# First attention of a two-layer kernel: fixed places for its small steps and long products

## The reference

```python
xn = _layernorm(x)
q, k, v = (split_heads(xn @ W.T) for W in (Wq, Wk, Wv))      # 8 batches, 16 heads, width 16
scores = jnp.where(causal, (q @ k.T) / sqrt(16), -inf)        # 512 x 512 for each head
x = x + (softmax(scores) @ v).reshape(8, 512, 256) @ Wo.T + ffn(xn)
```

## Time and profile before

| | |
|---|---|
| median of 3 runs | 1774.12 us (1771.36 to 1778.27) |
| profiled execution | 1778.4 us, span 1776.6 us |
| first attention, from scoresT of head 0 to the end of output | 64.8 to about 547 us |
| TensorE busy | 1613.5 us (91%) |
| VectorE busy | 863.5 us (49%) |
| ScalarE busy | 677.2 us (38%) |
| GpSimd busy | 741.4 us (42%) |
| mean granted TensorE clock | 0.961 |

### The profile page before, as it was taken

How to read it: one execution, slowest core, us unless ns; L and a number is a source line. 1 busy time by engine, 2 the same in 40 slices (tenths; PEclk the granted TensorE clock), 3 DMA queues, 4 the chain that set the end, 5 groups by cost and what they waited for, 6 DMA issues and landing times.

```text
span 1776.6 us, 32082 instructions
## 1 busy us (share of the span) xinstructions
PE 1613.5 (91%) x10912; PEld 1207.1 (68%) x10912; DVE 863.5 (49%) x2460; ACT 677.2 (38%) x1680; POOL 741.4 (42%) x845
## 2 busy tenths in 40 slices
PE   6888978888889999999896689998999999999997
PEld 3445434444446899999554456556899999999996
DVE  6777786657641322332264999886322122222221
ACT  4444434445462222222452334432433333333332
POOL 3122235545531455554621258785233333333332
PEclk9789989989999999999998799999999999999999
DMA  8434234353605122222531464464522222222221
GB/s 250 93 111 108 63 73 82 73 91 73 109 11 201 54 69 72 72 70 68 183 109 35 134 158 105 86 96 114 218 38 37 35 41 37 37 37 37 37 37 22
DMA packets 80027, 149.99 MB, mean 84 GB/s; under 512 B 13220, under 2 KB 61472, under 8 KB 73920
## 3 DMA queue, kind: packets, MB, share of 16 engines
q1 hardware_dynamic: 55328, 110.56, 24.6%
q0 software_dynamic: 24544, 37.38, 9.6%
HBM read 103.05 MB, written 44.45 MB: 83 GB/s over the span
## 4 chain that ended last, share of the span: by engine, by line
PE 78%; DVE 11%; issue 4%; ACT 2%; POOL 2%; DMA 1%; DVEq 0%; SPq 0%; ACTq 0%; POOLq 0%
PE PS L1488 22%; PE PS L1506 21%; PE PS L1366 4%; DVE PS L1793 4%; PE PS L1599 3%; PE PS L1302 3%; PE PS L1420 3%; PE PS L1462 2%; PE PS L1690 2%; PE PS L1330 2%; PE PS L1351 2%; PE PS L1473 2%; PE PS L1312 2%; PE PS L1392 2%; PE PS L1609 1%
## 5 line engine op out<-in xcount | busy, mean ns | idle before, releaser
L1488 PEld LDWEIGHTS PS<-arena 128*128 128x128 f32 x3408 | 398.3, 192 | 15.8 <-DVE arena L2016 4.5
L1488 PE MATMUL PS<-arena 128*128 128x128 f32 x3408 | 405.4, 276 | 3.1 <-DVE arena L2016 3.1
L1506 PE MATMUL PS<-arena 128*128 x1704 | 392.3, 379 | 0.0
L1506 PEld LDWEIGHTS PS<-arena 128*128 128x128 f32 x1704 | 311.6, 190 | 40.2 <-issue 0.2
L2016 DVE COPY arena<-PS 128x256 f32<-128x256 f32 x142 | 60.3, 424 | 413.0 <-PE PS L1473 402.6
L1793 DVE CUSTOM_DVE_ANT_0 PS<-PS,arena 128x512 f32<-128x512 f32 (+3 forms) x512 | 234.2, 524 | 39.5 <-PE PS L1330 39.2
L901 POOL DMA_INDIRECT out<-arena x71 | 111.6, 1572 | 314.0 <-ACT arena L1152 292.7
L1142 ACT ACTIVATE arena<-PS,arena 128x128 f32<-128x128 f32 x568 | 161.8, 368 | 138.2 <-PE PS L1488 138.2
L1077 ACT ACTIVATE arena<-PS 128x512 f32<-128x512 f32 (+1 forms) x256 | 167.2, 705 | 75.4 <-PE PS L1351 73.0
L841 POOL TENSOR_SCALAR_AFFINE_SELECT arena<-arena 128x256 f32<-128x256 f32 x256 | 98.5, 410 | 224.2 <-ACT arena L1077 223.2
L887 POOL DMA_INDIRECT arena<-XN,arena x142 | 142.1, 1001 | 102.7 <-PE PS L1473 64.5
(11 more groups left out here) (242 smaller groups left out, 2020.9 us busy)
## 6 DMA issues: line engine op xcount, KB each, us to landing
arena<-FD SPq DMA_DIRECT2D x32, 512.0 KB
arena<-in_w SPq DMA_DIRECT2D x16, 1024.0 KB
SPL<-arena SPq DMA_DIRECT2D x32, 384.0 KB, 2.6
arena<-SPL SPq DMA_DIRECT2D x30, 384.0 KB
XN<-arena SPq DMA_DIRECT2D x16, 512.0 KB, 3.2
arena<-SUM SPq DMA_DIRECT2D x16, 512.0 KB, 5.0
arena<-SPL SPq DMA_DIRECT2D x30, 256.0 KB
arena<-SPL SPq DMA_DIRECT2D x34, 128.0 KB, 3.9
```

The lines of the kernel that those rows point to most:

```text
L1488: ins = pe.matmul(o, m.now[i % 2][:, c * F + 128 * f:c * F + 128 * f + 128], m.xt[i % 2][:, 128 * c:128 * c + 128], start=(c == 0), stop=( ...
L1506: ins = pe.matmul(to, m.hT[i % len(m.hT)][:, 128 * c:128 * c + 128], m.WD[:, bass.ds(e * (nf * 256) + c * 256, 256)], start=(c == 0), stop ...
```

## The change

`attention_places()` gives each small step and each long product a fixed idx, and a side: 0 behind scoresT, 1 behind scores. The queue, its ranks and its pauses are gone. `values`, the stacks, the norm, the routing and the scatters stay where they were by idx, and the number of steps is the same.

In the old list, in the steady state, counting idx modulo 16: output twice at 2 (once on each side), project_v twice at 3, project at 5 and 6 and at 13 and 14 (side 1), scale at 1, 6, 9 and 14 (side 0), unscaleT at 2 and 10 (side 0), split and maxrow at 5 and 13.

```diff
+def attention_places():
+    places = {}
+
+    def put(idx, behind, *steps):
+        places.setdefault((idx, behind), []).extend(steps)
+
+    for n in range(2, NHB):
+        first = -LEAD if n == 2 else 8 * n - (22 if n % 2 else 18)
+        put(first, 1, ("project", n, 0))
+        put(1 - LEAD if n == 2 else 8 * n - 17, 1, ("project", n, 1))
+    for n in range(NHB):
+        put(8 * n - 3, 0, ("split", n))
+        put(8 * n - 3, 1, ("maxrow", n))
+        for g in range(2):
+            put(8 * n + 4 * g + 5, 1, ("scale", n, g))
+        put(8 * n + 10, 0, ("unscaleT", n))
+    for b in range(NB):
+        put(16 * b + 19, 1, ("output", b, 0))
+        put(16 * b + 22, 1, ("output", b, 1))
+        if b:
+            put(16 * b - 6, 1, ("project_v", b, 0))
+            put(16 * b - 5, 1, ("project_v", b, 1))
+    put(NH + 1, 1, ("shared_up", 0, 3), ("shared_gelu", 0, 3))
+    put(NH + 3, 1, ("shared_up", 1, 0), ("shared_gelu", 1, 0))
+    return places
...
-            step(False)
+        out += places.pop((idx, 0), [])
+        lead = idx + LEAD
         if lead < NH:
             out.append(("scores", lead // 8, lead % 8))
-            if lead % 8 == 7:
-                later(0, [("pause",), ("split", lead // 8), ("maxrow", lead // 8)])
-        step()
...
+        out += places.pop((idx, 1), [])
+        if idx == 2 - LEAD:
+            out.append(("stack", 2))
+        if 4 <= idx <= NH and idx % 4 == 0:
+            g = idx // 4 - 1
...
+            out.append(("values", g // 2, g % 2))
```

More of the change, by code:

```diff
@@ L54, in ln0_steps @@
             yield [(kind, b)]
-def attention_order():
[L59 to L80, removed]
+def attention_places():
[21 more added lines that the diff above has]
+    return places
+def attention_order():
+    out, places, ln = [], attention_places(), ln0_steps()
     out += [("stats", 0), ("root", 0), ("norm", 0), ("xt0", 0), ("xt1", 0), ("stats", 1), ("root", 1), ("norm", 1)]
@@ L85, in attention_order @@
     out += [("stats", 2), ("stats", 4), ("logits", 0), ("logitsT", 0), ("stats", 3), ("logits", 1), ("logitsT", 1), ("stats", 5)]
-    later(0, [("project", 2, 0), ("project", 2, 1), ("stack", 2)])
     route = iter([("route", p) for p in range(20)] + [("scatter", i, (k,)) for i in range(NT) for k in range(2)])
@@ L89, in attention_order @@
     lnleft = True
-    for idx in range(-LEAD, NH + 1):
-        if idx % 8 == 5 and 3 <= (idx + 3) // 8 + 2 < NHB:
-            later(0, [("project", (idx + 3) // 8 + 2, 0), ("project", (idx + 3) // 8 + 2, 1), ("pause",)])
+    for idx in range(-LEAD, NH + 7):
         if idx % 8 == 0 and 3 <= idx // 8 + 2 < NHB:
@@ L102, in attention_order @@
             out += [("shared_gelu", 0, fc) for fc in range(3)]
-        lead = idx + LEAD
         if idx == 0:
@@ L107, in attention_order @@
             out.append(("scoresT", idx // 8, idx % 8))
-            step(False)
+        out += places.pop((idx, 0), [])
+        lead = idx + LEAD
         if lead < NH:
             out.append(("scores", lead // 8, lead % 8))
-            if lead % 8 == 7:
-                later(0, [("pause",), ("split", lead // 8), ("maxrow", lead // 8)])
-        step()
[L114 to L123, removed]
+        out += places.pop((idx, 1), [])
[3 more added lines that the diff above has]
+            g = idx // 4 - 1
+            if g >= 2 * NHB - 2:
+                out.append(("shared_up", 0, g - 2 * NHB + 3))
+            out.append(("values", g // 2, g % 2))
         if lnleft:
@@ L131, in attention_order @@
             out += [s for s in [next(clears, None)] if s]
[L132 to L137, removed]
+    assert not places
     out += list(route)
@@ L140, in attention_order @@
     return out
-CLOSE = ("stack", "maxrow", "unscaleT", "pause", "done")
 def shared_order():
```

## The result

The changed kernel takes 1763.43 us (median of 20 runs, 1753.3 to 1772.32), the kernel before in the same comparisons 1773.96 (20 runs, 1769.1 to 1780.39). The ratio is 0.9942 [0.9925, 0.9958], a gain of 10 us (10.5 by the medians) or 0.6% (0.4 to 0.75%). That is faster by about the bound of 0.5%, inside the range, and **half of the 20 us forecast**.

The account below looks back on a forecast made before the run. The order of the work, no engine always busy, was taken as the bound. Six windows at 3.1 (18.6 us), first window 2, last 1.1, routing -2: 20 us less, 1754 against 1774.1; own range 1745 to 1764, full range 1732 to 1778.

Parts of the forecast that it names:

- The walk of the steps: Step-by-step sum over sixteen heads of the first attention: 51 us against 55.3 before, 4.3 us less.
- unscaleT at 2: At position 2, unscaleT would wait about 1.2 us for the scaled rows, since VectorE does the row maxima first.
- Output at 6: At position 6, output follows scale in bank 7 and would wait 0.4 us for VectorE's read.
- Values at 8: With no projection ahead in POOL's queue, its wait at position 8 would fall from 2.6 to about 0.35, worth 2.2 us.
- Values at 4: At position 4, values would wait 0.7 us for the low part of the projection at 2, masks queued behind it.
- bare sum of 50.4: Sum of the sixteen walked steps, in us, before adding 0.1 to 0.2 for steps with a projection, which gave 51.
- the term of the stack: Ahead of a group's first scores, late stacks would cost 1.2 us per sixteen heads; ends 0 and 4.4 + 3.1.
- the routing window: Window of the routing steps: VectorE, busy 56 of 66 us, can give back only half of the gain; -2 us.
- The first window: First sixteen-head window: would gain about 2 us, since project_v leaves a step of 6.5 us.
- the rival called halved: Waits on VectorE come out near 2 us, 4.3 becomes 2.3 or less, the whole 10 us: 1764 to 1768; chance 0.22.
- the third rival: Stacks land late for each odd group, 4.4 us of stall, clock halving behind each: about 1805; chance 0.14.
- The first rival, the clock: TensorE keeps 2.4 GHz with shorter waits; some 4 us more per window in five windows: 1734; chance 0.18.

Follow-up runs that it names:

- e_noscat: Changed kernel with the 64 scatters moved out of the attention loop to after it; 1810.89 us, one execution, only the windows are compared.
- the three other executions named above: Profiled executions of e_after, e_noscat and e_gap, whose order up to head 48 is the changed kernel's; first window 62.8, 63.1 and 61.4 us.
- e_gap_scale_low: Changed kernel with scatters kept out of stack steps, scale(n, 1) ahead of the scores, and q's low part behind the next head's masks; 1739.72 us, ratio 0.9833.
- e_before_noscat: Kernel before with the 64 scatters moved out of the attention loop to after it; 1835.12 us, one execution, only the windows are compared.
- e_scale0: Changed kernel with the second half-group's scale ahead of the scores again (positions 1 and 9); 1749.83 us, ratio 0.9876.
- e_gap: Changed kernel with no scatters in the three positions of eight where a stack is in flight, two in two others; 1747.11 us, ratio 0.9873.
- e_best: e_old_low_scale with scatters kept out of the steps in which a stack is read, and output's second half one step later; 1768.76 us, ratio 0.999.
- e_low: Changed kernel in which GpSimd makes the low part of q one step later, behind the next head's masks; 1762.76 us, ratio 0.9952.
- e_old_low_scale: Changed kernel with projections at their old places, scale(n, 1) ahead of the scores, and both low parts behind the next head's masks; 1769.28 us, ratio 1.0001.
- e_after: The changed kernel itself, run again beside a later batch; 1757.2 us (seven runs), ratio 0.9926.

## Why the prediction was right in sign and half in size

**The walk of the steps held, to 1 us.** Sum 51 forecast, 52.0 measured, against 55.3: 3.3 us and not 4.3. Without scatters the change is worth 3.4 to 5.9 per sixteen heads, but 1.7 to 3.4 of that is the clock, which the walk doesn't hold. The positions can be read in TensorE's timeline from position 2 to 10 of heads 48 to 63:

```profile
258.05 0.66 PE L1374 MATMUL PS<-arena 128*128 128x128 f32 x4 [1.14 <-DVE arena L1809]
...
261.90 1.90 PE L1384 MATMUL PS<-arena 128*128 128x256 f32 x8
263.63 0.71 PE L1343 MATMUL PS<-arena 99*128 99x512 bf16 x4
...
266.03 2.36 PE L1358 MATMUL PS<-arena 128*32 128x512 f32 x32 [1.08 <-POOL arena L833]
...
272.85 1.97 PE L1384 MATMUL PS<-arena 128*128 128x256 f32 x8 [0.38 <-DVE arena L1809]
...
277.47 0.71 PE L1343 MATMUL PS<-arena 99*128 99x512 bf16 x4
...
279.09 2.36 PE L1358 MATMUL PS<-arena 128*32 128x512 f32 x32 [0.36 <-DVE arena L1771]
```

- unscaleT at 2 waits 1.14 us for VectorE's scaled rows: forecast 1.2. Output at 6 waits 0.38 for its bank: forecast 0.4. Output at 3 waits for nothing.
- Values at 8 starts 1.62 behind its scoresT, the 0.36 in front of it is VectorE's read of the projection at 7: forecast 0.35 and "within 1.6".
- Values at 4 starts 2.40 behind its scoresT (263.63 to 266.03), where 1.9 was forecast, and at position 0 it is 2.6 and not about 2. These two waits on GpSimd, 1.1 us more together, make up the walk's error of 1.0. GpSimd's timeline shows the row that was left out of the term for position 4:

```profile
262.87 1.09 POOL L837 TENSOR_TENSOR arena<-arena 128x512 bf16<-128x512 f32 x1 [3.77 <-DVE arena L1773]
264.12 0.98 POOL L859 DMA_INDIRECT SLOT<-arena  x1 [0.15 <-issue]
265.11 0.77 POOL L833 TENSOR_SCALAR_AFFINE_SELECT arena<-arena 128x256 f32<-128x256 f32 x2
```

The low part, then a scatter's issue, then the masks: the same three as in the earlier trace rows. The forecast named the first and the third for this place, and not the second. e_noscat shows that this is the missing piece: without scatters the steps at 0 and 4 take 3.9 us each, and the windows 50.2 to 51.0, around the forecast's bare sum of 50.4.

**The step that failed most is the term of the stack.** It was set at 1.2 us per sixteen heads (its parts as given, 0.6, 0.1 and 1.3 for two groups of seven, come to about 1.1). In the four windows with scatters the waits are 17.6 and 15.7 us in two profiles against 6.1 before, so 2.9 and 2.4 more per sixteen heads. The term was 1.2 to 1.7 short there, and the one for GpSimd 1.0. The time available was right for odd groups: for group 9, 17.3 us from the start of the step after its projection (277.47) to 294.80, where 17.0 was forecast. For even groups it was 19.4 to 19.5, not 18.3, since values at 0 and 4 waited longer. The time needed was wrong in both of its parts:
- Landing was taken from group 15, 12.6 us as a bound from above and "less than its full length". Groups 8 to 15 are what it stood for, and they land in 12.1 to 18.3. That a group's scores wait for nothing bounds the landing for that group alone: in the kernel before, groups 8 to 15 landed in 12.6, 15.5, 12.3, 15.4, 12.3, 12.2, 14.7 and 12.2 us, and the 14.7 of group 14 was hidden by its slack.
- From an even group's projection to the first stack DMA it is 7.2 to 7.5 us in groups 8, 12 and 14 (6.2 in group 10), not 5.8. With the projection at 15, its low part comes behind the masks of the next head on GpSimd. The forecast counted on just that order for the gain at position 0 ("its low part is queued behind the masks that values needs"), and did not charge it to the stack.

The 15.6 us of group 9 before, which the forecast carried over for two groups of seven, were not simply a slow transfer. The earlier trace rows has the sign of it: its six issues take 5.00 us, those of group 15 take 2.70. One single issue lasted 2.8 us in place of 0.4, and the k half landed 11.9 us after its own first issue, against 10.9 for group 15. The same hold of 2.3 to 2.9 us stands in groups 11, 12 and 14 of that trace, and each of the four begins within 0.1 us of a packet of 16 KB on the profile's instruction queue, which lasts 2.0 to 2.5 us. That the packet is the cause is likely but wasn't tested. The changed kernel's profile has no such hold, and there the k half of group 9 took 16.8 us by itself. So the late stacks of these two profiles have different reasons, and the one could not give the size of the other.

**The accounting of a window.** For heads 48 to 95 the windows after are 61.8, 57.7 and 57.6: 52.0 of clean steps, 8.1, 3.75 and 3.3 of stack waits, and 1.7 to 2.3 for half clock behind these waits and small delays. Before, the same left 55.3, 3.0, 3.0 and 0, and 2.8 to 3.9. So of the 4.3 of the walk 1.0 was lost to GpSimd, some 3 were paid to the stacks, and some 1.5 came back, mostly since fewer stretches run at half clock. Heads 16 to 47, where no scatter runs, gained 3.4 and 5.5, more than the 3.1 and 1.1 forecast. In the second of them, the routing window, the granted clock rose from 0.92 to 0.97, which by an estimate from these two numbers and the windows' lengths may be 3.5 of the 5.5 us, so it doesn't decide whether VectorE kept half of the gain. The first window lost 0.6 where 2 was expected; the three other executions named above changed by -1.6 to +0.1, so none reached 2. The runs don't say why.

**The rivals.** The size is that of the rival called halved (1764 to 1768, measured 1763.4), its mechanism is not: no wait on VectorE came out above its forecast. It is the mechanism of the third rival, late stacks with half clock behind them, at under half of the price given to it: two groups of eight (9 and 11) pass the landing of 13.9 from which it outweighs the gain, not all. The first rival, the clock, is true in part. In heads 48 to 95 e_noscat and e_gap_scale_low stand at 1.00, e_before_noscat at 0.94 to 0.97: 1.7 to 3.4 us per window, where the rival said some 4. In the pair of profiled executions the time lost to half clock from head 0 to 111, taken as one less the granted clock times each window's length, is 30 us before and 22.5 after. This estimate counts idle time too, but the clock may be as much as half of the 15.7 us. The forecast had kept it out of its sum.

**What stays open.** Why the landings vary between 12.1 and 18.3 in one execution, why completions come up to 4 us behind the data, and why the late ones move from group to group between executions; why e_scale0 gained; why e_gap gained 10 us with stack waits of 14.3. A version with the maxrow DMA ahead of the write-out on SP, which e_best asks for, wasn't tried.

## What to carry to other kernels

A step moved closer to a transfer is paid for by the transfer's slowest case beside everything else that moves data at that time; read its length from all its instances, a late one above all, since an instance that nobody waits for only bounds its own length, and split a late one into issue, data and completion before it is carried over. Where a step is held back or moved, list every queue that takes its parts in order and what stands behind it in each, even if it belongs to another chain (here maxrow's DMA behind a write-out behind a low part). And before two good edits are added up, ask whether one of them takes away the slack on which the other lives: e_low gave its gain to the stacks, e_old_low_scale and e_best theirs to a queue.

## What the runs showed of the hardware

- Small indirect scatters, with 1.0% of the DMA engines' time and 0.01 MB in 22 us, made the read-back of a 1.5 MB stack beside them longer: 10.7 to 12.1 us without them (two kernels), 12.1 to 18.3 in the changed one, 12.2 to 15.5 in the kernel before. The Trainium skill's formula (DMA: Bandwidth & Descriptors, Anatomy of one DMA) is for one DMA issued by GpSimd; taken for the whole stack, as the prediction did, it gives 5.6 us by an estimate, about half of even the undisturbed case.
- A landing can end long after its data: 4.25 us between the last data packet (297.63) and the last increment of the semaphore (301.88), for group 9 of the changed kernel, 3.3 and 2.1 for groups 11 and 13, and again 4.3 and 3.0 for the two late groups of e_after; 0.5 to 1.4 without scatters.
- One DMA issue on SP took 2.76 us in place of 0.42 (before, 294.67), beside a 16 KB packet of the instruction queue that lasted 2.38 us; the same four times in that trace.
- TensorE ran at 1.2 GHz (1.23 us for scores and 1.25 for scoresT in place of 0.71) directly behind waits of 7.17, 3.58 and 3.33 us, and for a few us only. A wait of 2.24 us (416.56 of the changed kernel, scores in 1.23 us) was enough too. With no stack wait above 1.6 us the window of heads 64 to 79 of e_gap_scale_low had a granted clock of 1.00. Values at 385.50 of the changed kernel, behind the same wait of 1.09 as at 385.00 before, took 2.36 us and not 4.49:

```profile
385.50 2.36 PE L1358 MATMUL PS<-arena 128*32 128x512 f32 x32 [1.09 <-POOL arena L833]
```

So a wait of that length doesn't bring the half clock by itself. It isn't needed either: in e_before_noscat values at 346.19 took 4.06 us with no wait recorded ahead of it. What brought the half clock there isn't known.
